# Two leading FFN blocks of expert 0, filled from the first four batches and run beside the last routing work

## The chip, the cores and the metric

One NeuronCore of a Trainium2 chip runs the whole program. The metric is device time in microseconds. Engines have their own instruction streams and meet at semaphores: PE (TensorE, matmul), DVE (VectorE), ACT (ScalarE), POOL (GpSimd) and SP (SyncE, which here only issues transfers). Kernel before: 451.57 us, median of 3 runs (451.43 to 452.61).

## What is computed

x is (8, 256, 256) in float32, so 2048 tokens of width 256; the context is (8, 120, 256). First a gated cross-attention, then a gated mixture of experts, with top 2 of 8 experts:

```python
x = x + tanh(g_xattn[0]) * xattn(layernorm(x), ctx, Wq, Wk, Wv, Wo)   # 16 query heads, 4 kv heads, rope, mean over groups
h = layernorm(x)
probs = softmax(h @ gate_w.T); w, idx = top_k(probs, 2); w = w / sum(w)
for e in range(8):                       # gate_up_proj (8, 2048, 256), down_proj (8, 256, 1024)
    g, u = split(h @ gate_up[e].T, 2)
    acc += combine[:, e] * ((silu(g) * u) @ down[e].T)
x = x + tanh(g_ffn[0]) * acc
```

## The kernel before

**Attention and routing.** A loop over t = 0..8 works on one batch (256 tokens, two tiles of 128) per round, one stage behind the other: scores, softmax and values of batch t, projection, residual and choice of the two best experts of batch t-1. Batches are routed in sets, `SETS = ((0,1),(2,3),(4,5),(6,),(7,))`. For each set: `choose` (DVE) makes 0/1 picks, `ranks` (PE, small bf16 products with ones and a strict triangle) gives each pick its running number within its expert, `ranks_of_picks` and `slots` (DVE) turn that into a slot, the expert's range starting at e * CAP. `mark_slots` (DVE, one wide comparison) and `mark_places` (POOL for batches 0 to 5 and half of 6, DVE for the rest) build one-hot operands; `invert` (PE) multiplies them, so that afterwards each slot knows its token. Empty slots name a filler row. `second_norm` or `rstd_alone` with `shift_rows` make the second layernorm's scale and shift, `share_out` (POOL) the routing weights beside the row, and `store_rows` (SP) writes rows of a set to a scratch tensor in memory.

**Tables.** When the last ranks are known, DVE counts blocks of 128 slots per expert and builds five table columns (expert of each block, which weight pieces to convert after it, used or not, column of its token list). PE turns them into a row (L1025), DVE copies it (L1373, `tables_ready`), and all engines read their block's expert from it. `find_tokens` (L1232) makes the token list. TensorE does two idle products twice (`stay_warm`, L795) in this stretch.

**Expert blocks.** A block gathers 128 rows with an indirect DMA (`gather`, L513), applies the layernorm (`stage`, ACT), is transposed (`transpose_x`, L962) and split into a high and a low part (`x_high`, `x_low`), since float32 products are made from three fp32r ones. `expand` (L978) makes gate and up in two halves of 12 products, `gate` (Silu) and `product` the hidden row, `transpose_h` (L988), `h_high` and `h_low` its transposed parts, `contract` (L998) 12 products per half, `weigh` the weighting, and `scatter` (L520) adds 128 rows to the output. The order of a step is written out: on PE expand(s, 0), the rest of block s-1's first half, transpose_x(s+1), expand(s, 1), transpose_h(s, 0), contract(s-1, 1). Each engine runs a first step (s = 0), a loop of pairs, and then steps while the table says that a block is used. POOL gathers four blocks ahead.

**Weights.** Each expert has three pieces of 1 MB. SP loads a piece into `wraw`, ACT rounds its high part (`split_high`), POOL subtracts (`split_low`). Experts alternate between two places. The second place holds attention data and the one-hot operands until these have been used.

Of the kernel before, what the change touches and what calls it, by code (L numbers as in the profile page):

```python
# [40 lines left out]
NBLK = (2 * T + E * (P - 1)) // P  # L41
NCOL = NBLK + 5
FULL = 2 * T // P
PAIRS = (FULL - 1) // 2
# [22 lines left out]
NS = len(SETS)  # L67

# [7 lines left out]
BY_POOL = 2  # L76
# [22 lines left out]
def build_program(nc, x_d, xT_d, ctx_d, kvw_d, wq_d, wo_d, woT_d, gu_d, dn_d, const_d, out_d):  # L99
    rows_d = nc.dram_tensor("rows_scratch", (T + P, XW), F32, kind="Internal").ap()  # L100
    ctx = ExitStack()
    with ctx:
# [31 lines left out]
        first_silu = sb("first_silu", [P, 1])  # L134
# [24 lines left out]
        before_bf = sb("before_bf", [P, P], BF16)  # L159
        ones_bf = sb("ones_bf", [P, P], BF16)  # L160
# [62 lines left out]
        places.append(hT[:, 0, 0, 0:PICKS * P])  # L223
# [15 lines left out]
        tab_ps = misc[0:1, 0:5 * NCOL]  # L239
# [33 lines left out]
        loads_ended = sem("loads_ended")  # L273
        w_in = [sem(f"w_in{p}") for p in range(3)]
# [9 lines left out]
        block = ctx.enter_context(nc.Block())  # L284

# [32 lines left out]
        def _(sp):  # L318
# [27 lines left out]
            sp.dma_start(out_d[T:T + P, :], x_d[T:T + P, 0:D]).then_inc(zero_out, 16)  # L346
            sp.dma_start(rows_d[T:T + P, :], x_d[T:T + P, :]).then_inc(rows_filler, 16)
            out_v = out_d[0:T, :].rearrange("(t p) d -> p t d", p=P)
            rows_v = rows_d[0:T, :].rearrange("(t p) d -> p t d", p=P)
# [26 lines left out]
        def _(pool):  # L376
# [7 lines left out]
            nc.gpsimd.memset(spread[:, :, :, :], 1.0).then_inc(fills, 1)  # L384
            pool.sem_inc(y_free, RING)
# [75 lines left out]
            def mark_places(b, n):  # L461

                if b >= DEPTH:
                    pool.wait_ge(inverted, b - DEPTH + 1)
                for i in range(n):
# [3 lines left out]
                ins.then_inc(hits_ready, 1)  # L469

# [5 lines left out]
            for t in range(1, B + 1):  # L476
                if t in (2, 4):
                    score_scale(t + 2, 2)
                if t == B:
                    place_values(NS - 2)  # L480
                    mark_places(B - 2, BY_POOL)
                    rstd_alone(NS - 1)
                    share_out(NS - 2)
                elif t - 2 in ENDS:
                    place_values(ENDS[t - 2])
                    for b in SETS[ENDS[t - 2]]:
                        mark_places(b, PICKS)
                    share_out(ENDS[t - 2])
                if t == B - 1:
                    rstd_alone(NS - 2)  # L490
                elif t - 1 in ENDS and t < B:
                    second_norm(ENDS[t - 1])
# [6 lines left out]

            def column(s):  # L500
                return pool.value_load(tab[0:1, 4, bass.ds(s, 1)], min_val=0, max_val=SLOTS - 1)

            def keep_index(into, s, i):

                nc.gpsimd.tensor_copy(into[:, i:i + 1], token_at[:, bass.ds(column(s), 1)]).then_inc(index_kept, 1)

            def gather(s, q, index):

                if not isinstance(s, int) or s >= 2:
                    pool.wait_ge(x_staged, s - 1)  # L510
                    pool.wait_ge(weights_kept, s - 1)
                pool.sem_inc(index_settled, 1)
                nc.gpsimd.indirect_dma_start(out=xg[:, q, :], out_offset=None, in_=rows_d,  # L513
                                             in_offset=bass.IndirectOffsetOnAxis(ap=index, axis=0))                  .then_inc(x_loaded[q], 16)
# [22 lines left out]
            def step(s, r):  # L537
                middle_piece(s)
                pool.wait_ge(index_kept, s * 2 + 4)
# [5 lines left out]
                end_pieces(s)  # L545
# [3 lines left out]
            pool.wait_ge(token_at_ready, 1)  # L549
            pool.wait_ge(rows_filler, 16)  # L550
            pool.wait_ge(rows_out, 16 * NS)
            gather(0, 0, token_at[:, 0:1])
            pool.wait_ge(tables_ready, 1)
            keep_index(index_in, 1, 1)
            pool.wait_ge(index_kept, 1)
            gather(1, 1, index_in[:, 1:2])
            for s in range(2, RING):
                keep_index(index_in, s, s)
            nc.gpsimd.tensor_copy(index_out[:, 0:1], token_at[:, 0:1]).then_inc(index_kept, 1)
            pool.wait_ge(index_kept, RING)  # L560
            for s in range(2, RING):
                gather(s, s % 2, index_in[:, s:s + 1])
            end_pieces(0)
            keep_index(index_in, RING, 0)
            pool.wait_ge(index_kept, 5)
            gather(RING, 0, index_in[:, 0:1])
            keep_index(index_in, RING + 1, 1)
            pool.wait_ge(zero_out, 16)
# [3 lines left out]
            with pool.Fori(0, SURE) as i:  # L572
# [14 lines left out]
            steps_while_used(ROUNDS * RING + 1, 0, NBLK - 1 - ROUNDS * RING)  # L587
            last = pool.value_load(last_block[0:1, 0:1], min_val=FULL - 1, max_val=NBLK - 1)
            keep_index(index_out, last, RING)
            pool.wait_ge(index_kept, last * 2 + 7)  # L590
# [6 lines left out]
        def _(act):  # L597
# [67 lines left out]

            place_keys(0)
# [4 lines left out]
            for t in range(B + 1):  # L671
# [15 lines left out]
            nc.scalar.activation(first_silu[:, :], ones[:, 0:1], ACT.Silu)  # L687

            def stage(s, q):

                act.wait_ge(x_loaded[q], 16 * ((s >> 1) + 1))
                nc.scalar.activation(xs[:, :], xg[:, q, 0:D], ACT.Identity, scale=xg[:, q, D + RSTD:D + RSTD + 1],
                                     bias=xg[:, q, D + SHIFT:D + SHIFT + 1]).then_inc(x_staged, 1)
                nc.scalar.activation(meta[:, bass.ds((s & (KEEP - 1)) * META, META)], xg[:, q, D:D + META], ACT.Copy)\
                  .then_inc(weights_kept, 1)

            def x_high(s, par):
                act.wait_ge(xT_made, s + 1)
                nc.scalar.activation(xT[:, par, 0, :, :].rearrange("p c t -> p (c t)"), bank[7][:, 0:D],  # L699
                                     ACT.Copy).then_inc(xT_hi, 1)  # L700
# [25 lines left out]
            def step(s, par, first=False):  # L726
                gate(s, 0)
                if not first:
                    h_high(s - 1, 1)
                x_high(s + 1, 1 - par)  # L730
                stage(s + 2, par)
                if not first:
                    middle_piece(s)
# [4 lines left out]
            stage(0, 0)  # L738
            x_high(0, 0)
            stage(1, 1)  # L740
            act.wait_ge(tables_ready, 1)
            step(0, 0, first=True)
            with act.Fori(0, PAIRS) as i:
                step(i * 2 + 1, 1)
                step(i * 2 + 2, 0)

            def steps_while_used(i, u):

                s = i * 4 + (FULL - 1 + u)
                used = act.value_load(tab[0:1, 3, bass.ds(s, 1)], min_val=0, max_val=1)  # L750
                with act.If(used > 0):
                    step(s, (FULL - 1 + u) % 2)
# [3 lines left out]
            with act.Fori(0, (NBLK - FULL + 1) // 4) as i:  # L756
# [9 lines left out]
        def _(pe):  # L766
# [24 lines left out]

            def stay_warm(n):

                for _ in range(n):
                    nc.tensor.matmul(sc[:, 1, :], ident, const[:, 0:512], start=True, stop=True)  # L795
# [64 lines left out]
            def ranks(g):  # L860
# [4 lines left out]
                if g >= 1:  # L865
                    pe.wait_ge(slot_ready, g)
                pe.wait_ge(exp_done, TB * min(SETS[g][-1] + 3, B))
# [14 lines left out]
            def invert(b, first, last):  # L882
# [3 lines left out]
                if b < B - 1:  # L886
# [61 lines left out]
            pe.wait_ge(x2_ready, B)  # L948
            ranks(NS - 1)
            late = SETS[NS - 3][0]  # L950
            for b in SETS[NS - 3]:
                invert(b, late, B - 1)
            invert(B - 2, late, B - 1)
            invert(B - 1, late, B - 1)


            def transpose_x(s):
# [3 lines left out]
                for k in range(KC):  # L961
                    mm = nc.tensor.transpose(bank[7][:, k * P:(k + 1) * P], xs[:, k * P:(k + 1) * P], ident)  # L962
                mm.then_inc(xT_made, 1)

            def expand(s, par, hf, e):
# [7 lines left out]
                for k in range(KC):  # L973
                    for xp, wp in ((0, 0), (0, 1), (1, 0)):
# [33 lines left out]
            def step(s, par, first=False):  # L1008
                e = expert_of(s)
                expand(s, par, 0, e)  # L1010
                if not first:
                    e_before = expert_of(s - 1)
                    transpose_h(s - 1, 1)
                    contract(s - 1, 0, e_before)
# [3 lines left out]
                if not first:  # L1018
                    contract(s - 1, 1, e_before)

            pe.wait_ge(pT_copied, TB * B)
            stay_warm(1)
            pe.wait_ge(rows_tabled, 1)
            for k in range(5):
                mm = nc.tensor.matmul(tab_ps[:, k * NCOL:(k + 1) * NCOL], tab_rows[:, k:k + 1], ident[:, 0:NCOL],  # L1025
                                      start=True, stop=True)
            mm.then_inc(tab_psum, 1)
            stay_warm(1)
            transpose_x(0)
            pe.wait_ge(tables_ready, 1)  # L1030
            step(0, 0, first=True)
            with pe.Fori(0, PAIRS) as i:
                step(i * 2 + 1, 1)
# [494 lines left out]
```

## Time and profile before

| | |
|---|---|
| median of 3 runs | 451.57 us (451.43 to 452.61) |
| profiled execution | 451.98 us, span 450.2 us |
| mean granted clock | 0.949 |
| PE busy | 405.0 us (90%) |
| POOL, DVE, ACT busy | 258.7, 212.7, 205.3 us |
| gathers, scatters | 38 (one by the token list itself), 34 |

The page cuts the span into 40 slices of 11.25 us with the busy share of each in tenths. The chain of waits goes back from the last instruction to what released each step. Rows of a timeline give start, duration, engine, line and operation, and behind them in brackets how long the engine had been idle and what released it.

### The profile page before, as it was taken

Reading aid. Unit: us, or ns where it says so; the run is one execution under the profiler, and the core shown is the slowest. Engines: PE = TensorE matmul, PEld = TensorE weight load, DVE = VectorE, ACT = ScalarE, POOL = GpSimd, SP = SyncE. Lnnn points to the kernel's source line nnn. Section 1 sums busy time; section 2 is a strip of 40 time slices with the busy share of each in tenths; the row PEclk is TensorE's granted clock in tenths of the full one; section 3 lists DMA queues with packets and bytes.
Section 4 is the critical chain, followed back from the end, with each engine's and each line's share of the span. In section 5 each row is a group of like instructions: output and inputs, shape, how many; then the busy total and the mean of one; then the engine's idle time right before and its main releaser. Section 6 shows DMA issues by size and latency. Waiting matters only on the chain.

```text
span 450.2 us, 10881 instructions
## 1 busy us (share of the span) xinstructions
PE 405.0 (90%) x2476; PEld 339.6 (75%) x2477; DVE 212.7 (47%) x577; ACT 205.3 (46%) x453; POOL 258.7 (57%) x257
## 2 busy tenths in 40 slices
PE   6979677648999999999999999999999999999950
PEld 5645354444888888888888889888888888888850
DVE  2556997772344343443443544434434344444330
ACT  2569877121752356337336423563256336433310
POOL 3116679964386339728944953497239836953221
PEclk9999998855999999999999999999999999999985
DMA  8960122931055123612551541246114531112111
GB/s 270 402 260 25 43 77 83 315 123 37 14 180 160 26 33 118 211 37 40 193 138 26 187 140 24 35 133 206 24 24 116 169 90 24 24 26 42 33 27 12
DMA packets 19624, 46.66 MB, mean 104 GB/s; under 512 B 2368, under 2 KB 13760, under 8 KB 16512
## 3 DMA queue, kind: packets, MB, share of 16 engines
q1 hardware_dynamic: 11632, 35.18, 22.7%
q0 software_dynamic: 6720, 9.64, 11.8%
q10 hardware_dynamic: 1248, 1.57, 1.0%
q8 instruction: 9, 0.15, 0.1%
q14 instruction: 15, 0.12, 0.1%
HBM read 37.64 MB, written 9.00 MB: 104 GB/s over the span
## 4 chain that ended last, share of the span: by engine, by line
PE 72%; POOL 7%; DVE 3%; issue 1%; DMA 1%; POOLq 1%; ACT 0%; DVEq 0%; ACTq 0%
PE sc L978 21%; PE att L998 21%; PE misc L978 11%; PE qbank L978 11%; PE pT L988 6%; POOL dn L467 3%; PE att L962 2%; POOL dn L398 1%; DMA out<-xT_all,index_out 1%; POOL x L409 1%; POOL hT L467 1%; PE sc L795 0%; POOL out L520 0%; DVE stats L1068 0%; POOL vareps L407 0%
## 5 line engine op out<-in xcount | busy, mean ns | idle before, releaser
L520 POOL DMA_INDIRECT out<-xT_all,index_out x34 | 54.6, 1605 | 109.1 <-DVE xT_all L1406 101.0
L998 PE MATMUL att<-dn,hT 128*128 x816 | 115.2, 291 | 0.2 <-DVE hT L1384 0.2
L998 PEld LDWEIGHTS att<-dn,hT 128*128 128x128 f32 x816 | 102.7, 192 | 0.6 <-issue 0.5
L978 PE MATMUL sc<-gu,xT 128*128 x408 | 102.9, 401 | 0.0
L978 PEld LDWEIGHTS sc<-gu,xT 128*128 128x128 f32 x408 | 74.1, 188 | 15.0
L978 PE MATMUL misc<-gu,xT 128*128 x204 | 81.0, 397 | 0.8 <-ACT xT L699 0.8
L978 PE MATMUL qbank<-gu,xT 128*128 x204 | 80.9, 397 | 0.0
L392 POOL TENSOR_TENSOR gu<-wraw,gu 128x2048 f32 x14 | 64.5, 4625 | 9.2 <-ACT gu L615 7.1
L1380 DVE TENSOR_TENSOR xT_all<-xT_all,sc 128x512 f32<-128x512 f32 x34 | 23.4, 688 | 89.6 <-ACT xT_all L706 89.6
L706 ACT ACTIVATE xT_all<-misc 128x512 f32<-128x512 f32 x34 | 20.3, 597 | 73.8 <-PE qbank L978 73.8
L1380 DVE TENSOR_TENSOR xT_all<-xT_all,qbank 128x512 f32<-128x512 f32 x34 | 23.4, 688 | 64.0 <-ACT xT_all L706 64.0
L1384 DVE TENSOR_TENSOR hT<-pT,hT 128x512 fp32r<-128x512 f32 x68 | 46.5, 684 | 2.8 <-issue 2.8
L978 PEld LDWEIGHTS misc<-gu,xT 128*128 128x128 f32 x204 | 39.0, 191 | 8.5 <-issue 1.4
L513 POOL DMA_INDIRECT xT_all<-rows_scratch,index_in x37 | 36.7, 992 | 13.7 <-issue 10.1
L978 PEld LDWEIGHTS qbank<-gu,xT 128*128 128x128 f32 x204 | 39.0, 191 | 7.3
L988 PE MATMUL pT<-const,xT_all 128*128 128x128 f32 x272 | 40.8, 272 | 1.9 <-issue 1.9
L706 ACT ACTIVATE xT_all<-sc 128x512 f32<-128x512 f32 x34 | 20.3, 597 | 48.6 <-PE sc L978 48.6
L988 PEld LDWEIGHTS pT<-const,xT_all 128*128 128x128 f32 x272 | 33.9, 141 | 10.9 <-issue 2.1
L710 ACT ACTIVATE hT<-pT 128x512 fp32r<-128x512 f32 x68 | 40.3, 593 | 3.3 <-PE pT L988 3.3
L615 ACT ACTIVATE gu<-wraw 128x2048 f32 (+1 forms) x16 | 30.7, 1920 | 11.0 <-PE att L998 7.5
L392 POOL TENSOR_TENSOR dn<-wraw,dn 128x2048 f32 x7 | 32.3, 4609 | 0.0
L626 ACT ACTIVATE gu<-sc,shift,rs 128x120 f32<-128x120 f32 x64 | 27.9, 459 | 6.0 <-DVE shift L1107 5.9
(160 smaller groups left out, 472.8 us busy)
## 6 DMA issues: line engine op xcount, KB each, us to landing
wraw<-in_gu SPq DMA_DIRECT2D x16, 1024.0 KB, 5.5
wraw<-in_dn SPq DMA_DIRECT2D x8, 1024.0 KB, 5.1
x<-in_x SPq DMA_DIRECT2D x8, 266.0 KB, 11.7
xT_all<-in_xT SPq DMA_DIRECT2D x4, 512.0 KB, 11.3
out<-x SPq DMA_DIRECT2D x8, 256.0 KB, 3.4
rows_scratch<-x SPq DMA_DIRECT2D x3, 532.0 KB, 3.3
xT_all<-rows_scratch,index_in POOLq DMA_INDIRECT x37, 2.9
out<-xT_all,index_out POOLq DMA_INDIRECT x34, 3.9
```

The source lines that it names most:

```text
L392: nc.gpsimd.tensor_tensor(piece_of(where, 1, p), wraw[:, p * PIECE:(p + 1) * PIECE], piece_of(where, 0, p), ALU.subtract).then_inc(w_lo, 1)
L513: nc.gpsimd.indirect_dma_start(out=xg[:, q, :], out_offset=None, in_=rows_d, in_offset=bass.IndirectOffsetOnAxis(ap=index, axis=0)) .then_ ...
L520: nc.gpsimd.indirect_dma_start(out=out_d, out_offset=bass.IndirectOffsetOnAxis(ap=index, axis=0), in_=y[:, r, :], in_offset=None, compute_ ...
L615: nc.scalar.activation(piece_of(where, 0, p), wraw[:, p * PIECE:(p + 1) * PIECE], ACT.Copy).then_inc(w_hi, 1)
L626: ins = nc.scalar.activation(probs[:, b % 2, j, hh, :], score_ps(j, hh), ACT.Exp, bias=shift[:, hh // PAIR, j, hh % PAIR:hh % PAIR + 1], s ...
L706: nc.scalar.activation(silu[:, hf, :], bank[2 * hf][:, :], ACT.Silu).then_inc(silu_made, 1)
L710: nc.scalar.activation(hT[:, hf, 0, :], bank[4 + hf][:, :], ACT.Copy).then_inc(hT_hi, 1)
L978: mm = nc.tensor.matmul(bank[2 * hf + n][:, :], xT[:, par, xp, k, :], gu_part(where, wp, k * 2 * I + col, HALF), start=(k == 0 and xp == 0 ...
L988: mm = nc.tensor.transpose(bank[4 + hf][:, j * P:(j + 1) * P], h[:, hf, j * P:(j + 1) * P], ident)
L998: mm = nc.tensor.matmul(bank[6][:, 0:D], hT[:, hf, hp, j * P:(j + 1) * P], dn_part(where, wp, (hf * JH + j) * D, D), start=(hf == 0 and j ...
L1380: V.tensor_tensor(h[:, hf, :], silu[:, hf, :], bank[2 * hf + 1][:, :], ALU.mult).then_inc(h_made, 1)
L1384: V.tensor_tensor(hT[:, hf, 1, :], bank[4 + hf][:, :], hT[:, hf, 0, :], ALU.subtract)\
```

## The change

Slots of expert 0 that lie in its first two blocks are fixed once batches 0 to 3 (sets 0 and 1) are ranked. If these hold fewer than 256 picks of expert 0, the numbers up to 256 are skipped (`hole`), so that the two blocks are complete then. Their rows are gathered after set 1 is in memory, and the two blocks (`LEAD = 2`) are written out by hand on each engine among the last ranks, inversions and tables. Empty places now name row block 0, and tokens begin behind it, so a gather can be limited to the rows stored so far.

- POOL, t = 7: place_values, both gathers, then marks of batch 4, root of set 3, marks of batch 5, share_out. It marks no places of batch 6 any more.
- ACT: stage and x_high of block 0 and stage of block 1 come before the last `second_odds`; the early Silu on a dummy (`first_silu`) goes.
- PE: `stay_warm` goes; the order is given below.
- DVE: x_low(0) before the last `choose`; product(0, 0) before the table arithmetic, x_low(1) and product(0, 1) within it, h_low(0, 0) before the table copy.
- The table's row is taken in another PSUM bank; x of block 0 is transposed into bank 4; batch 3's and 7's marks lie in another part of hT.
- The block loop begins at s = 2. NBLK grows from 39 to 41, so the loop of possibly unused blocks has 3 rounds of 4, not 2, on PE, DVE and ACT.
- POOL converts expert 1's first pieces at fixed places instead of by table.

```diff
+LEAD = 2
+NBLK = (2 * T + LEAD * P + E * (P - 1)) // P
-PAIRS = (FULL - 1) // 2
+PAIRS = (FULL - LEAD) // 2
-                sp.dma_start(rows_v[:, a:z, :], x[:, a:z, :]).then_inc(rows_out, 16)
+                sp.dma_start(rows_v[:, a:z, :], x[:, a:z, :]).then_inc(lead_rows_out if g <= LEAD_SET else rows_out, 16)
...
 POOL
+            def gather_lead():
+                pool.wait_ge(lead_ready, 1)
+                pool.wait_ge(rows_filler, 16)
+                pool.wait_ge(lead_rows_out, 16 * (LEAD_SET + 1))
+                for s in range(LEAD):
+                    gather(s, s % 2, token_lead[:, s:s + 1], ready=S * (SETS[LEAD_SET][-1] + 1))
...
                 if t == B:
                     place_values(NS - 2)
-                    mark_places(B - 2, BY_POOL)
+                    share_out(NS - 2)
                     rstd_alone(NS - 1)
-                    share_out(NS - 2)
+                elif t == B - 1:
+                    place_values(NS - 3)
+                    gather_lead()
+                    mark_places(B - 4)
+                    rstd_alone(NS - 2)
+                    mark_places(B - 3)
+                    share_out(NS - 3)
...
 ACT
+                if t == B:
+                    stage(0, 0)
+                    x_high(0, 0)
+                    stage(1, 1)
...
             second_odds(NS - 1)
-            nc.scalar.activation(first_silu[:, :], ones[:, 0:1], ACT.Silu)
+            gate(0, 0)
+            x_high(1, 1)
+            gate(0, 1)
+            h_high(0, 0)
+            split_high(1, 0)
+            gate(1, 0)
+            h_high(0, 1)
+            split_high(1, 1)
+            stage(2, 0)
+            x_high(2, 0)
+            stage(3, 1)
+            gate(1, 1)
+            h_high(1, 0)
+            split_high(1, 2)
             act.wait_ge(tables_ready, 1)
...
 PE, ranks(g)
+                if g == LEAD_SET:
+                    pe.wait_ge(chosen_ready, g + 1)
+                    for t in range(z):
+                        nc.tensor.matmul(count_ps, ones_bf[:, :], chosen[:, t, :], start=(t == 0), stop=(t == z - 1))
+                if g > LEAD_SET:
+                    nc.tensor.matmul(out, ones_bf[:, :], hole_bf[:, :, :].broadcast_to([P, wide, E]), start=False, stop=False)
...
 PE
             pe.wait_ge(pT_copied, TB * B)
-            stay_warm(1)
...
             transpose_x(0)
+            expand(0, 0, 0, e, between=last_ranks)
+            pe.wait_ge(x2_ready, B)
+            for b in SETS[NS - 3]:
+                invert(b, late, B - 1)
+            pe.wait_ge(ends_read, 1)
+            expand(0, 0, 1, e)
+            invert(B - 2, late, B - 1)
+            invert(B - 1, late, B - 1)
+            transpose_x(1)
+            transpose_h(0, 0)
+            expand(1, 1, 0, e)
+            transpose_h(0, 1)
+            turn_tables()
+            contract(0, 0, e)
+            expand(1, 1, 1, e)
+            transpose_h(1, 0)
+            contract(0, 1, e)
             pe.wait_ge(tables_ready, 1)
+            transpose_x(2)
...
 DVE
+            def leave_hole():
+                link(V.tensor_scalar(hole[0:1, :], count_ps[0:1, 0:1], -1.0, float(LEAD * P), ALU.mult, ALU.add))
+                V.tensor_scalar(hole_bf[0:1, 0, 0:1], hole[0:1, :], 0.0, None, ALU.max).then_inc(hole_ready, 1)
...
+            mark_places(B - 2)
             shift_rows(NS - 1)
-            mark_places(B - 2, BY_POOL)
-            mark_places(B - 1, 0)
+            mark_places(B - 1)
             mark_slots(B - 1)
+            product(0, 0)
...
+            x_low(1, 1)
             find_tokens()
+            product(0, 1)
...
             dve.sem_inc(rows_tabled, 1)
+            h_low(0, 0)
             dve.wait_ge(tab_psum, 1)
             V.tensor_copy(tab[0:1, :, :], tab_ps.rearrange("o (k s) -> o k s", k=5)).then_inc(tables_ready, 1)
+            product(1, 0)
+            h_low(0, 1)
+            x_low(2, 0)
+            product(1, 1)
+            h_low(1, 0)
+            dve.wait_ge(tables_ready, 1)
+            weigh(0)
```

Between the two parts of `expand`'s first half (k = 0 and k = 1, six products each) stand the last ranks (`between`).

## Rows read from the trace of the kernel before

**Rows 1.** The page: slices of 11.25 us, and two groups of part 5.
```profile
PE   6979677648999999999999999999999999999950
PEclk9999998855999999999999999999999999999985
L1380 DVE TENSOR_TENSOR xT_all<-xT_all,sc 128x512 f32<-128x512 f32 x34 | 23.4, 688 | 89.6 <-ACT xT_all L706 89.6
L706 ACT ACTIVATE xT_all<-misc 128x512 f32<-128x512 f32 x34 | 20.3, 597 | 73.8 <-PE qbank L978 73.8
```

**Rows 2.** The chain of waits before the first block: start us, us, what.
```profile
84.41 7.40 POOL dn L467 x8
...
97.77 1.02 DVE hT L1211 x4
98.79 0.64 DVE dn L1195
...
101.25 0.36 DVE token_at L1232
...
103.67 0.89 PE misc L1025 x10
...
107.76 0.79 PE misc L978
```

**Rows 3.** The chain of waits in the first blocks.
```profile
110.26 0.43 PE qbank L978
...
112.51 2.77 PE sc L978 x12
...
120.55 2.78 PE sc L978 x12
...
125.20 0.23 PE misc L978
...
127.95 0.44 PE pT L988 x4
128.39 1.43 PE att L998 x12
...
130.04 2.78 PE sc L978 x12
```

**Rows 4.** SP's timeline, a transfer row (KB, us to landing), the gathers' landings.
```profile
81.94 0.37 SPq L356 DMA_DIRECT2D rows_scratch<-x  x1
...
rows_scratch<-x SPq DMA_DIRECT2D x1, 532.0 KB, 4.1
...
DMA to landing us min/median/max: 2.8/2.9/4.7
```

**Rows 5.** GpSimd's timeline, 92 to 108 us.
```profile
92.84 0.73 POOL L409 TENSOR_TENSOR x<-vareps,expo 128x2 f32<-128x2 f32 x1
...
102.56 1.23 POOL L513 DMA_INDIRECT xT_all<-rows_scratch,token_at  x1 [4.40 <-DVE token_at L1232]
...
106.96 0.98 POOL L513 DMA_INDIRECT xT_all<-rows_scratch,index_in  x1 [0.82 <-POOL index_in L505]
```

**Rows 6.** VectorE's timeline: first and last of seven in `choose`, tables.
```profile
90.63 0.18 DVE L1145 TENSOR_TENSOR ties<-ties,const 128x32 f32<-128x32 f32 x1
...
92.14 0.17 DVE L1157 TENSOR_TENSOR chosen<-route 128x16 bf16<-128x16 f32 x1
...
100.70 0.17 DVE L1343 TENSOR_SCALAR skip<-nblk 128x8 f32<-128x8 f32 x1
...
104.59 0.37 DVE L1373 CAST tab<-misc 1x220 int32<-1x220 f32 x1 [1.04 <-PE misc L1025]
```

**Rows 7.** ScalarE's timeline.
```profile
97.51 1.28 ACT L687 ACT_TABLE_LOAD   x1
```

**Rows 8.** The timeline of the tail, TensorE and GpSimd.
```profile
430.95 0.63 PE L988 MATMUL pT<-const,xT_all 128*128 128x128 f32 x4 [1.89 <-issue]
...
440.03 1.60 POOL L520 DMA_INDIRECT out<-xT_all,index_out  x1 [0.94 <-POOL index_out L505]
```

More of the change, by code:

```diff
@@ L67 @@
 NS = len(SETS)
+LEAD_SET = 1
+assert E * (P - 1) + LEAD * P < CAP and FULL % 2 == 0 and LEAD == 2
 PAIR = KVH // 2
@@ L535, in end_pieces, with step @@
                             split_low((v >> 3) + 1, p)
-            def step(s, r):
-                middle_piece(s)
-                pool.wait_ge(index_kept, s * 2 + 4)
+            def step(s, r, lead=False):
+                if not lead:
+                    middle_piece(s)
+                pool.wait_ge(index_kept, s * 2 + 3)
                 here, ahead = (r + 1) % RING, (r + 2) % RING
@@ L571, in _ @@
             SURE = (FULL - 1) // RING
-            with pool.Fori(0, SURE) as i:
+            for u in range(RING):
+                step(u + 1, u, lead=(u + 1 < LEAD))
+            with pool.Fori(1, SURE) as i:
                 for u in range(RING):
@@ L973, in expand @@
                 for k in range(KC):
+                    if k == 1 and between is not None:
+                        between()
                     for xp, wp in ((0, 0), (0, 1), (1, 0)):
@@ L1006, in expert_of, with step @@
                 return pe.value_load(tab[0:1, 0, bass.ds(s, 1)], min_val=0, max_val=E - 1)
-            def step(s, par, first=False):
+            def step(s, par):
                 e = expert_of(s)
                 expand(s, par, 0, e)
[L1011 to L1014, printed above, removed]
+                e_before = expert_of(s - 1)
+                transpose_h(s - 1, 1)
+                contract(s - 1, 0, e_before)
                 transpose_x(s + 1)
@@ L1017, in step @@
                 transpose_h(s, 0)
-                if not first:
-                    contract(s - 1, 1, e_before)
-            pe.wait_ge(pT_copied, TB * B)
-            stay_warm(1)
[L1023 to L1028, printed above, removed]
-            transpose_x(0)
+                contract(s - 1, 1, e_before)
@@ new lines, in last_ranks, with turn_tables @@
+            def last_ranks():
+                ranks(NS - 1)
+            def turn_tables():
+                pe.wait_ge(rows_tabled, 1)
+                for k in range(5):
+                    mm = nc.tensor.matmul(tab_ps[:, k * NCOL:(k + 1) * NCOL], tab_rows[:, k:k + 1], ident[:, 0:NCOL],
+                                          start=True, stop=True)
+                mm.then_inc(tab_psum, 1)
+            late = SETS[NS - 3][0]
+            pe.wait_ge(lead_expert_set, 1)
+            e = pe.value_load(lead_expert[0:1, 0:1], min_val=0, max_val=E - 1)
@@ L1205, in value_of_last, with mark_places @@
                     place[:, a:z, :], ALU.subtract))
-            def mark_places(b, first):
+            def mark_places(b):
                 dve.wait_ge(inverted, b - DEPTH + 1)
-                for i in range(first, PICKS):
+                for i in range(PICKS):
                     t, k = TB * b + i // 2, i % 2
@@ L1287, in _ @@
                     ranks_of_picks(ranked)
+                if ranked == LEAD_SET:
+                    leave_hole()
                 if t + 1 < B:
@@ L1308, in _ @@
                     add_residual(t - 1)
+                if t == B:
+                    x_low(0, 0)
                 if t < B:
@@ L1408, in step @@
-            def step(s, par, first=False):
+            product(1, 0)
[5 more added lines that the diff above has]
+            weigh(0)
+            def step(s, par):
                 product(s, 0)
-                if not first:
-                    h_low(s - 1, 1)
+                h_low(s - 1, 1)
                 x_low(s + 1, 1 - par)
```

259 lines of the change are left out of this document (126 added, 133 removed).

## The prediction

> **What bounds the kernel now.** I read the page's slices first [rows 1]: TensorE is at 9 tenths from about 113 us to the end, and weak in the slices from 79 to 113 us (6, 4, 8 tenths). In the last two of these the granted clock reads 5 tenths, its 1.2 GHz level; a product of 512 columns still takes 0.43 at 110.26, twelve take 2.77 at 112.51 [rows 3], so the clock came back near 111. Next the chain of waits, to see who sets that valley [rows 2]: GpSimd marks places for batches 4 and 5 (84.41 us, 7.40 us for 8 operations, 0.93 each), then VectorE marks the last batches until 99.43, builds tokens and tables, TensorE turns the tables at 103.67, and block 0's first expansion starts at 107.76. From there the chain is TensorE alone [rows 3]. One block is the distance between equal expansions, 130.04 - 120.55 = 9.49 us: twelve matrix products 2.77, four transposes 0.44, twelve contractions 1.43, each twice, and one transposition of x. So the kernel is a valley followed by 34 blocks at TensorE's rate.
>
> The yardstick: **block 2's first expansion starts at 125.20 [rows 3].** The changed kernel enters its loop at exactly this point (blocks 0 and 1 contracted or transposed as far as before), with the same blocks to come. Whatever it starts earlier is the gain.
>
> First, the number of blocks. This is not in the profile: I evaluated the reference's routing on its inputs. Experts receive 579, 508, 497, 586, 625, 504, 423 and 374 picks, so 5+4+4+5+5+4+4+3 = 34 blocks. Batches 0 to 3 hold 273 picks of expert 0, so the two leading blocks are full, no place stays empty, and there are 34 blocks after too.
>
> **The change, step by step.** Times are absolute in the profiled execution.
>
> 1. Rows of batches 2 and 3 are issued at 81.94 and take at most 4.1 us [rows 4]: all four batches are in memory at 86.0. The token list of the leading blocks costs one small VectorE operation beside add_places near 84 us and is ready earlier. `leave_hole` and the counting products lie at t = 5, while GpSimd, not they, sets the pace: nothing, at worst 0.4 us if that cover is gone.
> 2. GpSimd issues the gathers ahead of its marks. From the token list's end (101.25 + 0.36) to the gather's start were 0.95 us, and the issue took 1.23 and 0.98 for later ones [rows 5]. So: 87.0 to 88.2, second until about 89.5. A landing takes 2.8 to 4.7 us from the issue, median 2.9 [rows 4]. The last weight piece and output rows are in flight until about 90, so I take 4.5: 91.5. From landing to the first product: 107.76 - 102.56 - 3.0 = 2.2. Block 0's expansion starts at **93.7**.
>
> The Trainium skill (DMA: Bandwidth & Descriptors, "Anatomy of one DMA — SWDGE (gpsimd) path") fits 2.0 us plus bytes over 436 GB/s to one DMA; by it these 136 KB would take about 2.3 us. The trace's landings are 2.8 us at least [rows 4], so it disagrees for row gathers. By the page's figure the time would be some 2.2 us less than mine.
>
> 3. TensorE. At 1.2 GHz a product of 512 columns takes 0.43 [rows 3]: six are 2.6, to 96.3. The last ranks go between; eighteen small products, priced by the ten in 0.89 at 103.67 [rows 2], under 1 us: 97.2. Meanwhile VectorE, which now waits for x_low(0) before `choose`, ends that at 93.8 and the choice 1.68 later, 95.5 [rows 6]: in time. The other six products end at 99.8 (98.6 at full clock).
> 4. GpSimd from 89.5: marks of batch 4 in 3.7, square root of batch 6 about 1.1 [rows 5], marks of batch 5 in 3.7: 98.0. TensorE is there at 99.8, so they are no stall. Then row shares of two sets and the last square root, about 2.8 by the same row and the 1.76 us between the end of the marks and the end of that root (91.81 to 93.57): 100.8.
> 5. VectorE from 95.5: the work that before ran from the choice's end to the end of the last slots (92.31 to 99.43, 7.1 us with some 2 of waits), plus two marks that GpSimd did (0.26 each), with the new wait for the ranks: 103.1.
> 6. The table load before Silu, 1.28 us [rows 7], was hidden and no longer is: last odds at 101.4, load to 102.7, Silu 0.60 [rows 1] to 103.3. Product(0,0) takes 0.69 [rows 1]: 104.0. It stands ahead of the table arithmetic, and that is the real price of this order.
> 7. First table arithmetic, 99.43 to 100.88 before: 105.4. Then VectorE waits for block 1's x_low. On TensorE: inversion of batches 4 and 5 to 101.8, second half of block 0. Before, the clock read full 3.3 us after the solid work started (107.76 to 111). I take it as back near 101, so 2.8: 104.6; inversions of 6 and 7 to 105.7; transpose, high and low half of x to 106.9. Queued behind x_low(1) on VectorE are the token list (0.65), product(0,1) (0.69) and the second table arithmetic (101.61 to 103.67, 2.06): 110.3. Turning 0.6 (0.89 at half clock), copy 0.4: **tables ready at 111.4**, 6 us later than before (104.96) [rows 6].
> 8. From tables to the first indexed gather were 2.0 us [rows 5, 6], now with one more index copy: 113.5. Landing 2.9, then 2.2: block 2 expands at **118.6**. TensorE has 1.43 + 2.77 + 0.44 + 1.43 = 6.1 us of block 0 and 1 left after the turn, done at 117.0: here the gather is late, not TensorE, and 1.6 us stay empty.
> 9. Silu(1,1) is queued on ScalarE behind stage(2), x_high(2) and stage(3); with weigh(0) behind it on VectorE, so the first contraction of block 1 may find y_out late. No row shows this wait; its floor is nothing and its ceiling one Silu and two products (2.0 by rows 1). I take 0.5, an estimate nearer the floor, since the expansion of block 2 (2.77) covers most. Effective 119.1.
>
> Sum: 125.2 - 119.1 = 6.1 us gained. The tail: three used-block rounds instead of two on TensorE, VectorE and ScalarE. The present pass through such checks is an idle time of 1.89 us, but the end is set by GpSimd, whose last scatter starts at 440.03 after its own checks [rows 8]; its number of checks is unchanged. I book 0.1. Removing `stay_warm` gives nothing by itself. Result 451.98 - 6.0 = 446.0 for the profiled execution, which was 0.4 above the median 451.57: **445.6 us**.
>
> **Rivals.** Early: the first gather lands in 2.9 us (-1.6), the clock is back before the inversions so x_low(1) comes at 105.8 (-1.1), and no y_out stall (-0.5). For it: the marks of step 3 leave TensorE nearly solid. Against: transfers at that moment. 442.4 us.
>
> Clock late: full clock only when block 1 expands. The second half of block 0 costs 5.2, not 2.8, the inversions 2.0, x_low(1) is at 110.4, tables at 116.2, block 2 at 123.4. For it: the clock stayed low for two whole slices before [rows 1], across `stay_warm`. Against: there the gaps were far longer. 449.8 us.
>
> Clock never back in the lead (the slower side): after the turn at 117.6, the remaining products cost 12 instead of 6.1 us (0.43 each), so block 2 starts at 129.7: 4.5 us later than before, 456 us. It decides from where TensorE's work after the turn is still all at 1.2 GHz.
>
> GpSimd behind with the weights: splits of expert 1 come after four gathers, two of them in one step, so gather(6) is late for ScalarE's stage(6) near 141 us. I see about 1.7 us of slack; gone, it costs up to 3: 448.5 us.
>
> It doesn't do what it says: were there under 195 picks of expert 0 in batches 0 to 3, the filler would cost a block, 9.49: 455 us. My count of 273 all but excludes it.
>
> **Chances.** Forecast 0.58 (443.8 to 447.6), early 0.17, clock late 0.12, GpSimd behind 0.07, clock never back 0.05, extra block 0.01. The range reaches from the early case to the clock-late one: 441.8 to 449.8. About 0.3% is what a measurement here can tell from no change (450.2 to 452.9). Slower: the last two, 0.06. Same: a part of clock-late, 0.05. Faster 0.89.
>
> **What would show it.** First lead product near 93.7; its gather's landing over 3 us; Silu's table load near 101.4; tables copied near 111.4; block 2's expansion near 118.6 after an idle of 1 to 2 us on TensorE; 34 scatters; full clock from about 101 on. Wrong if the tables come before 108 or after 114, if the clock reads 5 tenths beyond 105, or if the distance between blocks is no longer 9.49.

## The result and the profile after

The changed kernel took 447.81 us (median of 6, 445.34 to 450.51) beside 452.09 (451.43 to 456.41). The ratio is 0.987, 95% interval 0.9836 to 0.9905, which lies clear of 1: faster, by 5.9 us if the ratio is taken of 452.09, while the two medians lie 4.3 us apart. The forecast was 6.0 us (445.6 from 451.57). Single executions of either kernel spread over 5 us, so small effects below are read in profiles, not in medians.

The profiled execution has a span of 446.4 us. The page's slices, which answer to [rows 1]:

```profile
PE   7977787668899999999999999999999999999840
PEclk9998898969999999999999999999999999999965
L1304 DVE TENSOR_TENSOR xT_all<-xT_all,sc 128x512 f32<-128x512 f32 x34 | 23.4, 688 | 84.2 <-ACT xT_all L736 84.2
L736 ACT ACTIVATE xT_all<-misc 128x512 f32<-128x512 f32 x34 | 20.4, 601 | 72.6 <-PE qbank L1012 72.6
```

The slices from 78 to 112 us read 6, 6, 8 where they read 6, 4, 8, but one of them has a clock of 6 tenths where two had 5, and the work in them now includes block 0's expansion and the first half of block 1's. TensorE's timeline through the lead (start, duration, line and operation, idle time and releaser in brackets), which answers to [rows 2, 3]:

```profile
89.38 1.13 PE L889 MATMUL att<-wo,oT 128*128 128x264 f32 x4
93.48 0.66 PE L994 MATMUL pT<-const,xT_all 128*128 128x128 f32 x2 [2.97 <-ACT xT_all L696]
95.00 0.79 PE L1012 MATMUL misc<-gu,xT 128*128 x1 [0.86 <-ACT xT L703]
...
97.84 0.53 PE L912 MATMUL sc<-chosen,ones_bf 128*128 128x24 bf16 x14
...
100.13 1.01 PE L931 MATMUL att<-dn 128*128 128x138 f32 x8
100.97 2.95 PE L1012 MATMUL sc<-gu,xT 128*128 x12
...
110.31 0.57 PE L1059 MATMUL att<-const,tab_rows 128*1 128x46 f32 x10 [0.66 <-DVEq L1477]
...
117.68 0.41 PE L994 MATMUL att<-const,xT_all 128*128 128x128 f32 x2 [0.21 <-issue]
119.09 0.50 PE L1012 MATMUL misc<-gu,xT 128*128 x1 [0.99 <-ACT xT L703]
```

Block 0 begins at 95.00, the second half of its expansion takes 2.95, as long as at full clock; the tables are turned at 110.31, and block 2 begins at 119.09 (forecast 118.6; before 125.20 in the chain, 125.04 in the timeline). ScalarE, GpSimd and VectorE, each from its timeline, answer to [rows 5 to 7]:

```profile
92.74 0.60 ACT L696 ACTIVATE xT_all<-xT_all 128x256 f32<-128x256 f32 x1 [7.14 <-DMA xT_all<-rows_scratch,token_lead]
...
102.24 0.48 ACT L690 ACTIVATE odds<-gaps,x 128x2 f32<-128x2 f32 x2 [6.50 <-POOL x L422]
102.74 1.28 ACT L736 ACT_TABLE_LOAD   x1
104.04 0.60 ACT L736 ACTIVATE xT_all<-misc 128x512 f32<-128x512 f32 x1
```

```profile
87.98 1.24 POOL L497 DMA_INDIRECT xT_all<-rows_scratch,token_lead  x1 [2.48 <-issue]
...
90.81 3.20 POOL L480 TENSOR_SCALAR dn<-const,slot_f,value 128x128 fp32r<-128x128 f32 x4
...
95.16 3.15 POOL L480 TENSOR_SCALAR dn<-const,slot_f,value 128x128 fp32r<-128x128 f32 x4
...
114.06 1.13 POOL L497 DMA_INDIRECT xT_all<-rows_scratch,index_in  x1 [0.85 <-POOL index_in L489]
```

```profile
92.65 0.68 DVE L1217 TENSOR_TENSOR x<-att,x 128x512 f32<-128x512 f32 x1
...
104.67 0.69 DVE L1304 TENSOR_TENSOR xT_all<-xT_all,qbank 128x512 f32<-128x512 f32 x1 [0.65 <-ACT xT_all L736]
...
110.95 0.38 DVE L1480 CAST tab<-att 1x230 int32<-1x230 f32 x1
```

ScalarE, which waits for the first gather's rows, starts 4.76 us after the gather's issue (87.98 to 92.74). The tail, timeline of TensorE, VectorE and GpSimd, answers to [rows 8]:

```profile
417.53 2.99 PE L1012 MATMUL sc<-gu,xT 128*128 x12
...
420.71 1.67 PE L1032 MATMUL att<-dn,hT 128*128 x12
...
429.35 1.09 PE L1022 MATMUL pT<-const,xT_all 128*128 128x128 f32 x4 [6.97 <-issue]
...
434.94 0.48 DVE L1330 TENSOR_SCALAR xT_all<-att,weight 128x256 f32<-128x256 f32 x1 [1.80 <-PE att L1032]
436.29 1.60 POOL L545 DMA_INDIRECT out<-xT_all,index_out  x1 [3.40 <-DVE xT_all L1330]
```

Here is the surprise. TensorE waits for nothing for 6.97 us between block 33's last products and the closing transposition, where it was 1.89 before, and the last scatter now waits for VectorE, which waits for TensorE.

**Where the time went.** Five marks cut both profiled executions into stretches: the residual of batch 7 (L1162 before, L1217 after), the second-half products of blocks 2 and 33, the last scatter, the end.

| stretch, us | before | after | difference |
|---|---|---|---|
| to the residual of batch 7 | 90.03 | 92.65 | +2.62 |
| to block 2's second half | 39.76 | 31.73 | -8.03 |
| blocks 2 to 33 | 294.39 | 293.15 | -1.24 |
| block 33 to the last scatter | 15.85 | 18.76 | +2.91 |
| to the end | 10.19 | 10.13 | -0.06 |
| span | 450.22 | 446.42 | -3.80 |

The first row varies by execution (experiments below). The other four sum to -6.4, and the ratios say -5.9 here and -6.4 when the kernel was run again, over 6 and 5 executions.

### The profile page after: what moved, and what is told of

Same layout as the page of the kernel before. It is cut to its first block, busy times and chain, and to the rows that moved or that the text cites. A ratio compares the mean times of both kernels' runs of the same rounds, so it can differ in the third digit from the quotient of the medians.

```text
span 446.4 us, 10758 instructions
## 1 busy us (share of the span) xinstructions
PE 401.8 (90%) x2483; PEld 338.9 (76%) x2484; DVE 212.8 (48%) x583; ACT 205.3 (46%) x452; POOL 257.1 (58%) x255
## 4 chain that ended last, share of the span: by engine, by line
PE 71%; issue 2%; ACT 1%; DVE 1%; POOL 0%; DVEq 0%; POOLq 0%; ACTq 0%
PE att L1032 22%; PE sc L1012 20%; PE misc L1012 10%; PE qbank L1012 10%; PE pT L1022 6%; PE att L994 2%; ACT xT_all L736 0%; POOL out L545 0%; ACT L736 0%; DVE xT_all L1304 0%; DVE hT L1308 0%; ACT hT L740 0%; DVE xT_all L1330 0%; ACT odds L690 0%; DVE xT L1297 0%
## 5 line engine op out<-in xcount | busy, mean ns | idle before, releaser
L1012 PE MATMUL sc<-gu,xT 128*128 x408 | 101.4, 397 | 0.0
L405 POOL TENSOR_TENSOR gu<-wraw,gu 128x2048 f32 (+1 forms) x14 | 64.4, 4619 | 1.1 <-issue 1.0
L1022 PEld LDWEIGHTS pT<-const,xT_all 128*128 128x128 f32 x272 | 33.8, 141 | 16.3 <-issue 7.1
L497 POOL DMA_INDIRECT xT_all<-rows_scratch,index_in x36 | 35.8, 995 | 13.2 <-issue 10.4
L405 POOL TENSOR_TENSOR dn<-wraw,dn 128x2048 f32 (+1 forms) x7 | 32.3, 4607 | 0.0
```

The lines of the kernel that those rows point to most:

```text
L405: nc.gpsimd.tensor_tensor(piece_of(where, 1, p), wraw[:, p * PIECE:(p + 1) * PIECE], piece_of(where, 0, p), ALU.subtract).then_inc(w_lo, 1)
L1012: mm = nc.tensor.matmul(bank[2 * hf + n][:, :], xT[:, par, xp, k, :], gu_part(where, wp, k * 2 * I + col, HALF), start=(k == 0 and xp == 0 ...
L1022: mm = nc.tensor.transpose(bank[4 + hf][:, j * P:(j + 1) * P], h[:, hf, j * P:(j + 1) * P], ident)
```

## The experiments

Theory one: the valley is won by the leading blocks as forecast, and the tail loses some 3 us to the loop of possibly unused blocks. Its rival: the tail's idle time is an accident, or comes from something else. Theory two: the later end of the attention stage is a cost of the counting and `leave_hole`. Its rival: the clock. Ratios are to the kernel before on the same chip, with 95% intervals.

**The changed kernel again.**

> The changed kernel once more, as the reference for the others of this chip. Expected about 0.987 of the kernel before, blocks about 9.45 us apart if that distance belongs to the program, about 9.49 if the chip of the earlier profile made it. Two theories of the stretch between block 33's last expansion and the next transposition on TensorE (6.97 us idle in its profile, 1.89 us before): if it belongs to the program it is there again within 0.5 us; if it was an accident of one execution it is near 2 us.

Ratio 0.9859 (0.9823 to 0.9895), 447.21 us. Idle time 6.85 us, blocks 9.456 apart, tables at 112.31, block 2 at 120.67. So both the idle time and the shorter distance belong to the program.

**Two rounds.** Block 40, which these inputs don't use, is left out.

```diff
-            with pe.Fori(0, (NBLK - FULL + 3) // 4) as i:      # and on ACT, DVE
+            with pe.Fori(0, 2) as i:
```

> The changed kernel with 2 instead of 3 rounds of four steps in the loop of possibly unused blocks on TensorE, VectorE and ScalarE (block 40 of 0 to 40, unused with these inputs, is left out). Theory A: the third, empty round costs TensorE one more jump back and forward and makes the tail's idle time 6.97 instead of 1.89 us; then the idle time falls to about 2, GpSimd sets the end again as before, and the time falls by about 3 us against the changed kernel (2.9 us were lost between block 33's expansion and the last scatter). Theory B: the idle time comes from leaving the round after its second step instead of after its third, whatever follows; then it stays near 7 us and the time is unchanged within 0.5 us.

Idle time and the last scatter of this kernel:

```profile
425.97 0.90 PE L1022 MATMUL pT<-const,xT_all 128*128 128x128 f32 x4 [3.72 <-issue]
...
433.67 1.60 POOL L545 DMA_INDIRECT out<-xT_all,index_out  x1 [0.94 <-POOL index_out L489]
```

3.72 lies between the theories (2 and 7). The third round is 3.1 to 3.3 us of the 6.97 and 6.85. The other 1.8 us (3.72 against 1.89 with the same two rounds) is what is left between the two kernels: one leaves the round after its second step, the other after its third. No run changed that place alone, so it isn't shown to be the cause. From block 33 to the last scatter 16.26 us, 2.5 less than in the changed kernel, and GpSimd's own index copy releases it again. The remaining 0.4 us against the kernel before is GpSimd's own: its last index copy starts 15.14 us after block 33's second half, and 14.72 in the kernel before. The profiled span is 443.8, but the median of 5, 448.1 (0.9879, 0.9842 to 0.9916), doesn't show it: that is inside the spread.

**Three rounds in the kernel before.**

```diff
-            with pe.Fori(0, (NBLK - FULL + 1) // 4) as i:      # and on ACT, DVE
+            with pe.Fori(0, 3) as i:
```

> The kernel before with 3 instead of 2 rounds of possibly unused blocks on TensorE, VectorE and ScalarE, nothing else. Theory A (an empty round costs TensorE about 5 us, of which GpSimd's own checks covered 2.9): TensorE's idle time goes from 1.9 to about 7 us and the time rises by 2 to 2.5 us. Theory B (the place of leaving the round): no change, idle time near 1.9 us.

```profile
433.20 0.63 PE L988 MATMUL pT<-const,xT_all 128*128 128x128 f32 x4 [3.40 <-issue]
...
440.61 1.60 POOL L520 DMA_INDIRECT out<-xT_all,index_out  x1 [0.94 <-POOL index_out L505]
```

Here the third round costs TensorE 1.5 us, not 5, and the stretch to the last scatter stays (15.69 against 15.85): ratio 0.9993 (0.9968 to 1.0019). My reading that an empty round has one price is wrong: 1.5 us in this kernel, 3.1 to 3.3 in the changed one. The two differ in the step behind which the round is left (third and second), but also in the code around it, and why one is dearer stays open. Cover by GpSimd is real: 1.5 us of TensorE cost nothing.

**No rounds on four engines.** Steps written out, each in the condition of the one before:

```diff
-            with pe.Fori(0, (NBLK - FULL + 3) // 4) as i:
-                steps_while_used(i, 0)
+            steps_while_used(FULL)                 # s = 32 to 40, nested; the same on ACT, DVE, POOL
```

> The changed kernel without loops over possibly unused blocks: their steps are written out, each inside the condition of the one before, on all four engines, so that one jump leaves them all. Theory A (rounds of empty checks are what costs): TensorE's idle time before the last transposition is at most 1.9 us, GpSimd makes one check fewer, so the last scatter starts 3 to 4.5 us earlier against block 33 than in the changed kernel: 3 to 4.5 us gained. Theory B (fetching instructions that lie far ahead is what costs): the one jump over seven unused steps costs as much as the rounds did, and the time is unchanged or worse by up to 1 us.

The chain of waits in its tail, on GpSimd's queue:

```profile
428.34 0.15 POOLq L604
428.48 0.03 issue
428.53 0.03 issue
428.56 0.04 POOLq L605
428.61 2.76 issue
431.37 0.29 POOLq L611
```

TensorE's idle time is 3.57: neither at most 1.9, as theory A has it, nor what the rounds cost (near 7), as theory B has it. And now GpSimd stands 2.76 us at its one jump over seven unused steps. The last scatter starts 16.86 after block 33, 1.9 us less than in the changed kernel, not 3 to 4.5; 446.17 us, 0.9839 (0.9803 to 0.9874). Rounds and far jump both have a price on TensorE: the jump costs less than three rounds and about as much as two (3.72).

**No rounds on three engines,** GpSimd as in the changed kernel.

> The changed kernel with the possibly unused blocks written out without loops on TensorE, VectorE and ScalarE, GpSimd's rounds left as they are. Theory A (GpSimd, which in the kernel with all four written out stood 2.76 us at one far jump, then sets the end): the last scatter starts about 16.3 us after block 33's second-half products begin, as in the kernel with two rounds, 0.5 less than with all four written out and 2.5 less than in the changed kernel. Theory B (TensorE's own idle time sets it): it stays at 16.9 or more.

```profile
425.48 0.63 PE L1020 MATMUL pT<-const,xT_all 128*128 128x128 f32 x4 [3.33 <-issue]
...
432.94 1.60 POOL L545 DMA_INDIRECT out<-xT_all,index_out  x1 [0.94 <-POOL index_out L489]
```

15.63 us from block 33 to the last scatter, 3.1 less than in the changed kernel, and less than the 16.3 that theory A gave; GpSimd's index copy releases the scatter, so theory B falls. **444.56 us, ratio 0.9788 (0.9751 to 0.9826)**: the lowest median measured, and clearly below the kernel before. Against the changed kernel the tail's 3.1 us is what the profile shows. The intervals of the ratios just touch (the changed kernel's begin at 0.9836 and 0.9823, on other chips), and the next two kernels, with the same edit, come to 0.9811 and 0.9819.

**GpSimd's wait at the head of the next step, in the kernel before.** One more edit writes the first round out, so that no wait is on zero.

```diff
             def step(s, r):
+                if not (isinstance(s, int) and s == 1):
+                    pool.wait_ge(y_added, (s - 1) * 16)
+                    pool.sem_inc(y_free, 1)
                 middle_piece(s)
...
-                pool.wait_ge(y_added, 16 * s)
-                pool.sem_inc(y_free, 1)
...
+            pool.wait_ge(y_added, last * 16)
+            pool.sem_inc(y_free, 1)
             scatter(last, 0, index_out[:, RING:RING + 1])
```

> The kernel before, in which GpSimd waits for the landing of a scatter (and frees its place in y) at the head of the next step instead of at the end of its own, so that its checks for used blocks run during the landing; the first round is written out. Theory A (GpSimd's own checks after the landing set the end of the kernel before, with about 2.9 us of cover for TensorE's idle time): the last scatter starts about 2 us earlier against block 33 (13.8 instead of 15.85 us after it) and the time falls by about 2 us. Theory B (the landing itself, or TensorE, sets it): no change.

```profile
440.89 0.18 POOL L505 COPY index_out<-token_at 128x1 int32 x1 [3.05 <-issue]
441.24 0.48 DVE L1411 TENSOR_SCALAR xT_all<-att,weight 128x256 f32<-128x256 f32 x1 [2.28 <-POOLq L595]
442.58 1.60 POOL L520 DMA_INDIRECT out<-xT_all,index_out  x1 [1.51 <-DVE xT_all L1411]
```

15.28 us, 0.57 less, not 2; ratio 0.9967 (0.9939 to 0.9994), 1.5 us, of which the tail shows only that 0.57. From the scatter before the last one to the last index copy GpSimd now takes 6.27 us instead of 7.39 (434.62 to 440.89; before 431.51 to 438.90), so running the checks during the landing saves 1.12. But the edit also puts the release of the place in y (the buffer that a scatter reads; `y_free`) behind the checks: VectorE's last weighting now waits for it, and the last scatter waits for VectorE, 1.69 behind the index copy instead of 1.13. That gives half of the gain back. TensorE's idle time 1.92, blocks 9.496 apart: again the program's.

**All three edits on the changed kernel:** steps written out on three engines, GpSimd's wait at the head of the next step, and block 2's gather ahead of block 3's index copy. The cut shows the third.

```diff
             for s in range(LEAD, RING):
                 keep_index(index_in, s, s)
-            pool.wait_ge(index_kept, 3)
-            for s in range(LEAD, RING):
+                pool.wait_ge(index_kept, s)
                 gather(s, s % 2, index_in[:, s:s + 1])
```

> The changed kernel with three edits: possibly unused blocks written out on TensorE, VectorE and ScalarE; GpSimd's wait for a landing at the head of the next step; block 2's gather issued as soon as its own index is copied, ahead of block 3's. Expected if TensorE's idle time and GpSimd's checks were what the tail lost: the last scatter starts 14.8 us after block 33's second half (18.8 in the changed kernel), gain 4; and if the gather ends last ahead of block 2, tables to block 2's first product shrink from 8.1 to 7.5 us. Together 4.5 us under the changed kernel. Rival: the gather was not last (8.1 stays) and the tail is bound by the landing of the scatter before (16 us): 2.5 us.

The table copy at 112.83, block 2 at 120.46: 7.63 us where the changed kernel has 8.14 and 8.36, so block 2's gather did end last. To the last scatter 15.31. The time, 446.19 (0.9811, 0.9776 to 0.9846), is no better than with one edit; the intervals overlap.

**Closing products behind each check on TensorE,** on top of the three edits.

```diff
                 used = pe.value_load(tab[0:1, 3, s:s + 1], min_val=0, max_val=1)
+                with pe.If(used < 1):
+                    end_with(s - 1)
                 with pe.If(used > 0):
```

> The kernel with these three edits, and on TensorE the closing products of the last block written right behind each check, so that it need not jump over unused steps first. Theory A (the idle time of about 3.5 us ahead of the last transposition is the far jump): it falls below 1.5 us, and the last scatter starts 1.5 to 2 us earlier than with three edits, until the scatter before it has landed: 5.5 to 6.5 us under the changed kernel, about 0.973 of the kernel before. Theory B (it is the check itself, the load of the flag and the branch, wherever it leads): idle time near 3.5 us again, no gain.

```profile
424.03 0.60 PE L1022 MATMUL pT<-const,xT_all 128*128 128x128 f32 x4
...
427.40 0.60 ACT L742 ACTIVATE hT<-pT 128x512 fp32r<-128x512 f32 x1 [3.96 <-issue]
...
429.47 0.69 DVE L1311 TENSOR_TENSOR hT<-pT,hT 128x512 fp32r<-128x512 f32 x1 [3.98 <-issue]
...
433.26 0.48 DVE L1333 TENSOR_SCALAR xT_all<-att,weight 128x256 f32<-128x256 f32 x1 [1.75 <-POOLq L619]
```

On TensorE the idle time is gone, as theory A has it: it was the way over unused steps, not the check. But ScalarE and VectorE have an idle time of 4 us of their own, which TensorE's had hidden, and behind them VectorE waits for GpSimd, which frees the place in y only behind its own checks, as in the kernel before with the same deferral. So GpSimd sets the end, and the scatter starts 15.29 after block 33 (15.31 without this edit): no gain, 446.56 us (0.9819, 0.9782 to 0.9857).

**A mark ahead of the gathers.** `mark_places(B - 4)` moved ahead of `gather_lead()`.

> The changed kernel with GpSimd marking batch 4 (3.2 us) ahead of the two leading gathers instead of behind them. Theory A (the gathers are the head of the chain into the lead, the marks have slack): block 0's first product starts about 1.5 to 2 us later (the marks start at 85.5 while the rows land near 87.2, so part of the 3.2 is hidden), and the time rises by about 1.5 us. Theory B (GpSimd's marks of batches 4 and 5 end last in the lead, as they did before the change): earlier marks shorten the lead or leave it, time lower by up to 1 us or unchanged.

The gather is issued 2.4 us behind the residual of batch 6 (1.1 and 3.1 in the changed kernel's two profiles), and ScalarE starts on its rows 3.50 after the issue (4.76 and 3.76). From the end of the attention stage to block 2's second half 31.43 us against 31.73 and 32.15; ratio 0.9884 (0.9848 to 0.992). Neither theory's gain or loss shows, and 1 us could not show here: the same stretch took 30.45, 30.26 and 30.32 us in the kernels with two rounds and with steps written out on four and on three engines, whose work in it is the changed kernel's. What going first is worth stays below what these profiles tell apart.

**Moments of batch 7 ahead of the last ranks.** `second_moments(B - 1)` moved ahead of `ranks_of_picks(NS - 1)`.

> The changed kernel with the moments of batch 7 on VectorE ahead of the last ranks (where VectorE sits idle 1.8 us) instead of behind value_of_last. Theory A (the chain last odds, table load, Silu, product(0,0) sets the table arithmetic): the last odds on ScalarE start about 2.5 us earlier (99.7 instead of 102.2), product(0,0) about 1.5 us earlier, the tables and block 2 about 1 us earlier; time lower by 0.5 to 1.2 us. Theory B (TensorE's second half of block 0 and the inversions set block 1's x_low, and that sets the tables): odds earlier, tables within 0.3 us, time unchanged.

The table load starts 8.49 us after block 0's first product (7.74 and 7.82 in the changed kernel), the tables 16.70 after it (15.95 and 16.04); ratio 0.9893 (0.9861 to 0.9924). Theory A falls: the moments are ready at 98.9, but the root that the odds need stands behind GpSimd's marks and shares and starts at 102.94. A closer pair says the same: with all steps written out, the table copy comes 16.13 us after block 0's first product with this edit and 15.97 without.

**No counting and no hole.** The `leave_hole` call, its wait and the products on `hole_bf` and `count_ps` taken out.

> The changed kernel without the eight counting products, the two small VectorE operations of leave_hole, the wait for the picks ahead of them and the products that add the hole (left out: filling places up to 256, which these inputs don't need). Theory A (no cover at t = 5): the routing stage is 0.5 to 0.8 us shorter, and so is the time. Theory B (GpSimd sets the pace at that point, as forecast): no change within 0.3 us.

From the residual of batch 3 to that of batch 4 8.02 us; the changed kernel had 8.05 in an execution with the clock's dips at the same places, and the kernel before 8.02. From the residual of batch 0 to that of batch 7 it is 55.96 against 56.06. Theory B: these parts cost nothing that shows here. Ratio 0.9907 (0.9877 to 0.9937).

**Both, steps written out on four engines and moments.**

> The changed kernel with both: possibly unused blocks written out without loops on all engines, and the moments of batch 7 ahead of the last ranks. If both of the first theories hold, the gains add: 3.5 to 5.5 us below the changed kernel, some 9.5 to 11 us below the kernel before (0.976 to 0.979). If neither, it equals the changed kernel (0.987).

446.07 us, 0.9848 (0.9816 to 0.988): as with four engines written out (0.9839), the moments add nothing.

## Why the prediction was right, and where it was not

The direction and the stage were right, and so was the size: 5.9 us by the ratio for 6.0, 4.3 by the medians, 447.81 us for 445.6. That the ratio comes within 0.1 us is partly luck, since three errors cancel: against the forecast the valley gave 1.9 us more (8.03 for 6.1, with the attention stage's end as the mark) and the blocks 1.2, and the tail took 2.8. Block 0 started 2.35 us after the residual of batch 7 where the sum had 3.7, the way from there to the tables was 1.75 shorter, and the way from the tables to block 2 was 0.9 longer: 2.2 us in all, near the 1.9. In absolute time block 2 started 6.0 us earlier in this pair of profiles, with the attention stage's later end in it.

- **Steps 1 and 2.** Landing 4.5 us forecast, 4.76 measured; block 0 at 93.7 forecast, 95.00 measured. The attention stage ended 2.6 us later in this profile, which more than covers the difference. Taking the counting and the hole out of that stage changes nothing, and a variant of the kernel before (the deferred wait) had its batch-7 residual at 94.10, too: its granted clock fell to half in other places than in the profile before. Shifts of this size were missing from my sum. All profiles of the new order have that residual between 92.65 and 95.73, the three of the old order at 90.03, 91.24 and 94.10; whether the change makes the late ones more frequent stays open. That the ratios are as large as the last four rows of the table alone speaks against it.
- **Steps 3 to 7.** From block 0's first product to the table copy 17.7 us forecast, 15.95 and 16.04 measured. GpSimd's marks took 0.80 each, not 0.93. The clock was back at 99.0 in this profile, 4 us after block 0's first product, not at 101: a product is 0.63 at 97.29 and 0.39 at 99.20. In the second profile of the kernel it came back at 101.5, 5 us after that product (96.27). The order was right: last odds, table load, Silu, product(0,0), table arithmetic.
- **Step 8.** Block 2 at 118.6 forecast and 119.09 measured, 8.14 after the tables where I had 7.2: two index copies stood ahead of its gather, 3.11 from the table copy to the gather's start. Gathering for block 2 as soon as its own index is copied took 0.5 us off, which shows that this chain ends last.
- **Step 9.** The wait for y_out didn't come: TensorE stood idle for 0.13 us ahead of the contraction, with nothing to wait for, and 0.5 was booked.
- **The tail is the step that failed.** I booked 0.1 for a third round since GpSimd set the end. The stretch grew by 2.9. TensorE's idle time grew by 5.1 us, and GpSimd's cover was only about 2: in the profile before, VectorE's last weighting ended at 437.15 and the scatter started at 440.03, while 0.87 lay between the two where the scatter waits for it (435.42 to 436.29 after). With two rounds, or with none on three engines, 2.5 and 3.1 came back.
- **Blocks.** I took 9.49 as a constant. As a mean to block 33 it is 9.496 in three profiles of kernels with the old loop and 9.45 to 9.46 with the new one: 1.24 us that I hadn't. It lies in the second half of the expansion (2.86 against 2.82 us to the next transposition, in each block). Its cause stays open.

Of the rivals, neither the early nor the late case happened as a whole (one part of the early case did in the first profile: the clock was full before the inversions, which began at 100.13); GpSimd kept up with the weights; 34 scatters were run.

## What to carry to other kernels

A loop bound raised for generality is part of a change's price even if the extra rounds are empty: read the idle time "issue" in the tail, on each engine, and ask how much of it another engine covers. Hiding one engine's idle time at a jump shows only when the other engines' are taken away too. For work moved into a valley, count from the transfer's landing under the traffic of that moment, and judge effects of 1 or 2 us by stretches between marks of the trace, not by medians. Take several profiles for it: the lead's own stretch took 30.3 to 32.2 us with the same work.

## What the runs showed of the hardware that I had not expected

- Empty rounds and far jumps: leaving the loop took TensorE 1.89 to 6.97 us: 1.9 and 3.4 for two and three rounds in the kernel that leaves behind the third step, 3.7 and 6.9 in the one that leaves behind the second. With the same number of rounds both pass the same number of checks. A jump of GpSimd over seven steps took 2.76 us, of ScalarE and VectorE 4.0. That instructions are fetched late there fits. The DMA view of the tails has two queues called instruction (q8 and q14). In the changed kernel q8 moves one packet at 421.5 and one at 425.0 us, just ahead of TensorE's idle time and within it (422.4 to 429.35), and with the closing products behind each check, where that idle time is gone, none between 417 and 432. Which engine a queue serves and what a packet costs no run here shows.
- The same gather of 128 rows took 4.76, 3.76 and 3.50 us from its issue to the engine that waits for it, in kernels that issued it at 87.98, 90.34 and 89.67 us, each time with a weight piece issued some 4 to 5.5 us before. In the kernel with two rounds, issued at 88.47, it was 3.87: the time of issue alone doesn't order them.
- The distance between blocks, for the same products, differed by 0.4% or more between the old order and the new (9.496 against 9.447 to 9.460 us), in every profile taken of the one or the other.
